# Sorted blocks loaded for two steps at a time into three places, and chosen steps in pairs

## The reference, cut to what matters

```python
h = _layernorm(x, axis=-1) * (1 + ca) + sa
x = x + ga * _L0_attn_ref(h, ...)
h = _layernorm(x, axis=-1) * (1 + cb) + sb
x = x + gb * _L0_ffn_ref(h, ...)

# _L0_ffn_ref, T = 2048 tokens of 128, 160 experts of 64
probs = jax.nn.sigmoid(x @ router_w.T + expert_bias[None, :])
top_w, top_idx = jax.lax.top_k(probs, 8)
top_w = top_w / (jnp.sum(top_w, axis=-1, keepdims=True) + 1e-09) * 2.5
combine = jnp.zeros((T, 160)).at[jnp.arange(T)[:, None], top_idx].set(top_w)
h1 = jax.nn.silu(jnp.einsum('th,eih->eti', x, w_gate))
routed = jnp.einsum('eti,ehi->th', h1 * combine.T[:, :, None], w_down)
shared = jax.nn.silu(x @ w_gate_shared.T) @ w_down_shared.T
```

## Time and profile before

| | |
|---|---|
| time, median of 3 runs | 882.31 us (877.73, 882.55, 882.31) |
| profiled execution, its time | 883.9 us |
| its span | 882.1 us |
| TensorE busy (matmuls) | 777.3 us, 88% |
| VectorE, ScalarE, GpSimd busy | 557.9, 462.4, 548.7 us |
| chain that ended last, by engine | PE 45%, POOL 16%, DVE 12%, issue 10%, ACT 10%, DMA 4%, SPq 2% |
| its largest lines | POOL wT L1370 12%, PE ps L652 10%, PE ps L639 9% |
| block loads by ScalarE (L1285) | 26 of 512 KB, median 6.2 us to landing |
| mean granted TensorE clock | 0.957 of full |

### The profile page before, as it was taken

One profiled execution on the slowest core, in us unless ns is written; L12 is line 12 of the kernel. 1 busy time (PEld: TensorE's weight loads), 2 busy tenths in 40 slices (PEclk: granted clock), 3 DMA queues, 4 the chain that ended last, 5 costly groups with the idle time before them and its releaser, 6 DMA issues.

```text
span 882.1 us, 14173 instructions
## 1 busy us (share of the span) xinstructions
PE 777.3 (88%) x4386; PEld 494.9 (56%) x4386; DVE 557.9 (63%) x1394; ACT 462.4 (52%) x965; POOL 548.7 (62%) x418
## 2 busy tenths in 40 slices
PE   4789999999989999989999887796967799799992
PEld 2556666666656666656655555444856685344440
DVE  5876676777677787677887777432432334566665
ACT  3666666666666556766767770331543444233330
POOL 0588888898878787778775783761000004777774
PEclk9899999999999999999999999686998989999997
DMA  7986958665547656445344568866999976688872
GB/s 231 244 220 179 259 131 232 187 198 151 136 121 224 183 151 163 117 109 146 90 122 123 182 216 311 265 177 239 316 386 313 384 242 200 152 192 187 188 175 57
DMA packets 81018, 174.20 MB, mean 197 GB/s; under 512 B 12448, under 2 KB 30432, under 8 KB 78640
## 3 DMA queue, kind: packets, MB, share of 16 engines
q1 hardware_dynamic: 66256, 129.96, 53.1%
q10 hardware_dynamic: 8544, 30.74, 9.4%
q0 software_dynamic: 6144, 12.60, 5.4%
HBM read 96.83 MB, written 45.48 MB: 161 GB/s over the span
## 4 chain that ended last, share of the span: by engine, by line
PE 45%; POOL 16%; DVE 12%; issue 10%; ACT 10%; DMA 4%; SPq 2%; DVEq 0%; POOLq 0%; ACTq 0%
POOL wT L1370 12%; PE ps L652 10%; PE ps L639 9%; ACT prob L1099 5%; POOL sorted_rows L1328 4%; PE ps L628 4%; PE ps L630 4%; PE ps L602 3%; PE ps L970 3%; PE ps L992 3%; PE ps L1010 3%; DVE prob L1486 3%; DMA strips<-in_expert_rows 2%; PE ps L665 2%; PE ps L613 1%
## 5 line engine op out<-in xcount | busy, mean ns | idle before, releaser
L1312 POOL TENSOR_SCALAR prob<-prob,rinv 128x512 f32<-128x512 f32 x215 | 336.6, 1575 | 101.7 <-DVE rinv L1504 99.1
L1099 ACT ACTIVATE prob<-prob,nmax 128x512 f32<-128x512 f32 x256 | 183.0, 716 | 151.2 <-DVE nmax L1486 150.7
L1370 POOL DMA_INDIRECT wT<-sorted_rows,dest x96 | 106.3, 1107 | 169.6 <-DMA sorted_rows<-prob 140.7
L1486 DVE CUSTOM_DVE_ANT_0 prob<-ps,strips 128x512 f32<-128x512 f32 x256 | 164.9, 681 | 0.9 <-issue 0.2
L639 PEld LDWEIGHTS ps<-ident,prob 128*128 128x128 f32 x1024 | 114.5, 140 | 78.9 <-POOL prob L1312 37.6
L345 DVE COPY PT<-ps 128x512 f32<-128x512 f32 x128 | 88.2, 689 | 110.8 <-PE ps L639 109.4
L639 PE MATMUL ps<-ident,prob 128*128 128x128 f32 x1024 | 136.6, 276 | 6.1 <-ACT PT L345 5.4
L652 PE MATMUL ps<-PT,v_sb 128*64 128x512 f32 x512 | 123.8, 605 | 12.9 <-ACT PT L345 12.9
L1328 POOL DMA_INDIRECT sorted_rows<-xn,dest x96 | 100.4, 1046 | 33.6 <-issue 33.6
L628 PE MATMUL ps<-stack 128*128 128x512 f32 x256 | 114.1, 446 | 6.8 <-DVE nmax L1486 6.5
L1232 ACT ACTIVATE strips<-ps 128x512 f32<-128x512 f32 x80 | 47.8, 597 | 103.9 <-PE ps L1025 103.8
(11 more groups left out here) (269 smaller groups left out, 1145.9 us busy)
## 6 DMA issues: line engine op xcount, KB each, us to landing
stack<-qk SPq DMA_DIRECT2D x128, 256.0 KB
sorted_rows<-in_zero_rows SPq DMA_DIRECT2D x16, 1024.0 KB, 5.7
wT<-sorted_rows ACTq DMA_DIRECT2D x26, 512.0 KB, 6.2
sorted_rows<-prob ACTq DMA_DIRECT2D x22, 512.0 KB, 5.7
qk<-comb_rows SPq DMA_DIRECT2D x40, 256.0 KB, 4.2
strips<-in_expert_rows SPq DMA_DIRECT2D x96, 96.0 KB, 3.6
k_low<-qk SPq DMA_DIRECT2D x64, 128.0 KB
hT<-qk SPq DMA_DIRECT2D x64, 128.0 KB
```

Source lines behind the costliest of these rows:

```text
L1099: nc.scalar.activation(prob[:, u, :], prob[:, u, :], ACT.Exp, bias=nmax[:, u:u + 1], scale=-1.0, accum_out=rsum[:, u:u + 1]).then_inc(s_ex ...
L1312: nc.gpsimd.tensor_scalar(prob[:, u, :], prob[:, u, :], rinv[:, u:u + 1], None, ALU.mult).then_inc(s_prob, 1)
L1370: nc.gpsimd.indirect_dma_start(picked[:, n % NGATHER, k, :], None, sorted_rows, bass.IndirectOffsetOnAxis(ap=dest[:, n, k:k + 1], axis=0)) ...
L1486: nc.vector.tensor_tensor_reduce(out=prob[:, u, :], in0=ps[:, BANK_S + u % 2, :], in1=backwards, scale=-1.0, scalar=3.0e38, op0=ALU.add, o ...
```

## The change

A load now brings the blocks of two steps, 2u and 2u + 1: 16 blocks, 8 KB a partition, 1 MB. `x_blocks` has three places of that size in place of six of half of it, in the same memory. SyncE issues three loads in place of six; ScalarE issues 13 in place of 26, each at the odd step 2u' + 1 whose transposes free the place. Since the blocks of both steps must be neighbours, chosen steps stand in pairs: 4, 5, 10, 11, 14, 15, 20, 21, 24, 25, 30, 31 in place of 4, 6, 9, 11, 14, 16, 19, 21, 24, 26, 29, 31. The stores stay one for each step, and the weights' four places stay. SyncE's loop goes by `CHOSEN`, so the loads of chosen weights move with it.

```diff
--- before.py
+++ after.py
@@ -67,7 +67,7 @@
 BLOCKS = E + EXTRA
 KNOWN_STEPS, CHOSEN_STEPS = E // STEP, EXTRA // STEP
 NSTEPS = KNOWN_STEPS + CHOSEN_STEPS
-CHOSEN = [4 + 5 * k // 2 for k in range(CHOSEN_STEPS)]
+CHOSEN = [s + i for s in (4, 10, 14, 20, 24, 30) for i in range(2)]
 
 
 def step_blocks():
@@ -77,7 +77,7 @@
 
 
 STEPS = step_blocks()
-NX, NCHOSEN, NY, NGATHER = 6, 4, 3, 6
+NX, NCHOSEN, NY, NGATHER = 3, 4, 3, 6
 LATE = (0, 1, 2, 3, 14, 15, 16, 17)
 RANK_UNIT = 512
 FILLS = {2: 1, 3: 1, 4: 0, 5: 0, 6: 1, 7: 2, 8: 1, 9: 1}
@@ -268,7 +268,7 @@
         scaled = prob[:, 5, :]
 
         x_flat = wT[:, :, :].rearrange("p a n -> p (a n)").bitcast(F32)
-        x_blocks = x_flat.rearrange("p (r w d) -> p r w d", r=NX, w=STEP)
+        x_blocks = x_flat.rearrange("p (r w d) -> p r w d", r=NX, w=2 * STEP)
         picked = x_flat.rearrange("p (r k d) -> p r k d", r=NGATHER, k=TOPK)
         xT = v_sb[:, :, :, :].rearrange("p a t n -> p a (t n)")
         hidden = oT
@@ -491,10 +491,10 @@
                     sp.dma_start(chosen_weights[:, k % NCHOSEN, j * 192:(j + 1) * 192],
                                  expert_rows[bass.ds(expert * P, P), :]).then_inc(s_chosen[k % NCHOSEN], 16)
 
-            def load_blocks(s):
-
-                first, _ = STEPS[s]
-                sp.dma_start(x_blocks[:, s % NX, :, :], block_rows[:, first:first + STEP, :]).then_inc(s_x[s % NX], 16)
+            def load_blocks(u):
+
+                first, _ = STEPS[2 * u]
+                sp.dma_start(x_blocks[:, u % NX, :, :], block_rows[:, first:first + 2 * STEP, :]).then_inc(s_x[u % NX], 16)
 
             def load_spread(i):
 
@@ -959,15 +959,16 @@
 
             def transpose_blocks(s):
 
-                r = s % NX
-                pe.wait_ge(s_x[r], 16 * (s // NX + 1))
+                u = s // 2
+                r = u % NX
+                pe.wait_ge(s_x[r], 16 * (u // NX + 1))
                 for half in range(2):
                     if s == 0:
                         pe.wait_ge(s_by_dve, routed(2, RANKED1))
                     else:
                         pe.wait_ge((s_xa, s_xd)[half], s)
                     for j in range(4):
-                        last = nc.tensor.transpose(ps[:, XT[half], j * P:(j + 1) * P], x_blocks[:, r, 4 * half + j, :],
+                        last = nc.tensor.transpose(ps[:, XT[half], j * P:(j + 1) * P], x_blocks[:, r, s % 2 * STEP + 4 * half + j, :],
                                                    ident[:, :])
                     last.then_inc(s_xt, 1)
 
@@ -1278,18 +1279,18 @@
                 act.wait_ge(s_yd, s + 1)
                 act.dma_start(block_rows[:, first:first + STEP, :], y_blocks[s % NY]).then_inc(s_y[s % NY], 16)
 
-            def load_blocks(s):
-
-                first, _ = STEPS[s]
-                act.wait_ge(s_xt, 2 * (s - NX + 1))
-                act.dma_start(x_blocks[:, s % NX, :, :], block_rows[:, first:first + STEP, :]).then_inc(s_x[s % NX], 16)
+            def load_blocks(u):
+
+                first, _ = STEPS[2 * u]
+                act.wait_ge(s_xt, 4 * (u - NX + 1))
+                act.dma_start(x_blocks[:, u % NX, :, :], block_rows[:, first:first + 2 * STEP, :]).then_inc(s_x[u % NX], 16)
 
             for p in range(IN_FRONT):
                 dense_silu(p)
             copy_transposed(0)
             for s in range(NSTEPS):
-                if s + NX < NSTEPS:
-                    load_blocks(s + NX)
+                if s % 2 == 1 and s // 2 + NX < NSTEPS // 2:
+                    load_blocks(s // 2 + NX)
                 block_silu(s)
                 if s >= 2:
                     store_blocks(s - 2)
```

## The result

| us | before | after |
|---|---|---|
| median of 20 runs each | 882.39 (877.73 to 887.07) | 885.62 (882.11 to 892.42) |
| profiled execution, its span | 883.9, 882.1 | 883.98, 882.1 |
| ratio after / before, 95% interval | | 1.0041 (1.0023 to 1.0059) |

The kernel became 3.6 us slower, with an interval of 2.0 to 5.2 us. Forecast were 883.0 in a range of 877 to 890, and no change within 1%: both hold.

The account below looks back on a forecast made before the run. SyncE's row of weight issues was taken to bound the steps. Start +1.3, three more issues +0.3 and one load less in front -0.6 gave +1.0 us on the median 882.3: 883 us, range 877 to 890.

Parts of the forecast that it names:

- Weights in pairs, step 24: Gate 24 waits for SyncE's 46th weight issue in place of the 43rd: +0.3 us, bounds -1.2 and +4.5.
- Start: First block load, now 1 MB, lands later and moves SyncE's row by as much: +1.3 us, bounds 0 and +1.9.
- Fewer loads in front: One ScalarE block load, 0.52 MB, less ahead of the weights at step 24: -0.6 us, bounds 0 and -1.3.
- Longer rows: Block loads with 8 KB a partition in place of 4 move no faster: 0, give or take 0.7 us.
- Steps 15 and 25, 30 and 31: Weights for 15 and 25 cost nothing; step 30 needs the 62nd issue, taken as 0, at most +1.4 us.
- two waits for chosen weights remain: Sign on TensorE: waits for chosen weights at steps 14 and 24 only.
- Waits that could appear: Block loads issued 5 steps, 14.7 us, ahead still fit; short waits for stores stay covered ahead of step 24.
- Starved weights: Rival: ScalarE's 8 KB packets take 28% of SyncE's queue turns, +6.6 us on its row; 895 us in all, chance 0.12.
- the three issues of the pair not covered (+4.5): Part of the starved rival's sum: three more weight issues ahead of step 24, in full, +4.5 us.
- Spine relieved: Rival: fewer, larger packets unblock SyncE, issues at 1.3 us in place of 1.50, step 24's wait ends; 875 us, chance 0.06.
- the gathers: Sign: GpSimd's gathers behind the steps start at 738 to 740 us.
- the end of the wait at step 24: Sign: the second wait for chosen weights, at step 24, ends at 705 to 708 us.

Follow-up runs that it names:

- run 4: Kernel before with the eight loads of combine rows moved from step 6 to step 26, behind the chosen weights: 873.25 us, ratio to before 0.9911.
- run 5: Changed kernel with the eight loads of combine rows moved from step 6 to step 26: 879.39 us, ratio to before 0.9981.
- run 7: Kernel before with 32 of the 64 weight loads, every second chosen step's, issued by GpSimd: 876.99 us, ratio to before 0.9949.
- run 8: Changed kernel with the same 32 of the 64 weight loads issued by GpSimd: 878.44 us, ratio to before 0.9971.
- run 11: Kernel before with combine rows loaded at step 26 and every second set of chosen weights issued by GpSimd: 863.93 us, ratio to before 0.9813.
- run 12: Changed kernel with combine rows loaded at step 26 and every second set of chosen weights issued by GpSimd: 865.11 us, ratio to before 0.9824.
- run 1: Kernel before with only the chosen steps changed to pairs, block loads still 0.5 MB: 885.04 us, ratio to before 1.0041.
- run 9: Kernel before with chosen steps 6, 16 and 26 moved one step earlier, to 5, 15 and 25: 884.52 us, ratio to before 1.0035.
- run 2: Changed kernel with each 1 MB load issued as two of 0.5 MB, 4 KB rows, same places and moments: 885.83 us, ratio to before 1.0046.
- run 3: Changed kernel with SyncE loading all eight weights of a pair's first step ahead of the second's: 885.24 us, ratio to before 1.0048.
- run 6: Changed kernel with the third and fifth pairs two steps later, at 16, 17 and 26, 27: 886.3 us, ratio to before 1.0057.
- run 10: Kernel before with chosen steps 9, 19 and 29 moved one step later, to 10, 20 and 30: 882.14 us, ratio to before 1.0014.

## Why the prediction was right, and which step of it failed

Right was the reading of what bounds the kernel: SyncE's row of issues decides when gate 24 opens, and all behind it follows. Experiments 4, 5, 7, 8, 11 and 12 show it, each by relieving that row; 4 and 5 take 2 MB out of the full queue besides, and in 7 and 8 the weights get a queue more, so the row is the simplest reading and not the only one for each run alone. Right were the range and "no change within 1%". The point was near by some luck: the range is 13 us wide and held the upper bound of the term that failed as well, and in the profiles a start that came out 1.5 us shorter in place of 1.3 longer hid a part of it. One term of the sum was mis-sized, and two small ones had no effect that a run shows.

**Weights in pairs, step 24: +0.3 taken, +4.0 measured.** The step said "late issues land fast, because the queue is drained while TensorE stands", and let the 46th issue land in the 3.3 us that it took before. Those 3.3 us belonged to an issue for which nobody waited: TensorE had been standing since 699.9 us, ScalarE's last transfer, a load of 0.5 MB, was issued at 699.9, and the 46th came at 702.5. In the profile after, ScalarE issued a load of 1 MB at 699.0 and a store of 0.5 MB at 700.1, the 46th came at 701.1, and TensorE stood only from 702.1. So the queue was not drained in front of it. It lands like its predecessor in that place did: 7.0 us, as the 43rd before; in experiments 1 and 9 its gate follows it by 6.4 and 7.6. With the landing alike, three more issues cost 3 x 1.3 = 3.9 us. That was the upper bound of the same paragraph ("three more issues at 1.50 us, none covered, +4.5"), with the pace of 1.3 us that the 43rd to the 46th show. Runs 1, 2 and 9 put it somewhat lower: gate 24 stands 2.9 to 3.3 us later behind line 480 than before.

**Start: +1.3 taken.** The first wait grew by 1.0 us, from 3.77 to 4.77. It was not passed on. Gates 0 and 2 stand 7.63 us apart in the profile after and 10.13 in that of before: TensorE was granted its full clock earlier, and the stretch came out 1.5 us shorter. Experiment 1, which leaves the start as it was, has the ratio of the whole change; with an interval of 2.2 us on the difference, time alone excludes neither 0 nor +1.3. The fourteen profiles say more. In the seven of kernels whose first transpose waits for the whole first 1 MB (after and runs 2, 3, 5, 6, 8 and 12) the stretch to line 480 takes 26.5 to 28.5 us, 27.1 in the mean; in the other seven 25.4 to 28.2, 27.5 in the mean. So nothing of the longer wait is seen at the end of this stretch. Gates 0 and 2 stand 7.5 to 7.9 us apart in six profiles, five of them of the first group, and 9.4 to 10.2 in the other eight: the full clock came early more often where the wait was longer. Why stays open.

**Fewer loads in front: -0.6 taken.** At step 24, for which it was taken, the landing did not become shorter: 7.0 us after, where run 1, with the same pairs and loads of 0.5 MB, has 6.4. In the 3 us ahead of the 46th issue ScalarE issued 1.5 MB, where it was 0.5 MB before. Nothing in the runs shows this term.

**Longer rows: 0 taken.** Rightly 0 in the time; runs 1 and 2 say so. From 603 to 606 us, in the first loads, the profiles of before and after have 422 and 426 GB/s, from 640 to 656 us 384 and 388. The 407 GB/s of the earlier trace rows were moved by block loads alone: only 17 of the 168 packets of that stretch have under 2 KB, so they say nothing of transfers of 96 KB, which the prediction names beside them; where weights moved too, from 640 to 656 us, the rate was 384. The Trainium skill ("DMA: Bandwidth & Descriptors", section Bandwidth) asks for 1 MiB or more in one transfer; here, with several in flight, 0.5 MB and 1 MB give the same time.

**Steps 15 and 25, 30 and 31: no cost.** That holds: no gate after 24 waited, and run 10 finds no cost in 30. **Step 20 was left out of the working**, and a wait of 3.84 us appeared there: its first loads moved back with the pair, and the 30th issue came at 680.2 us. It lies ahead of step 24 and fits into its slack, and run 1 without it has the same ratio. The sign "two waits for chosen weights remain" failed by it: there are three.

**Waits that could appear.** No transpose waited for a block after the first, so five steps ahead of its use were enough: ScalarE's 13 loads landed after 6.9 us in the middle, 11.0 at most.

**The rivals.** *Starved weights* named the mechanism that is there (1026 turns in place of 1294, an issue held for 4.76 us), and gave it a price of 6.6 us that it has not: the delay of 3.7 us at the 14th issue is still 3.6 at the 30th and shrinks to 1.2 at the 40th. These ten issues took 12.8 us in place of 15.2, in the time in which TensorE stood at step 20, and not at step 14. Whether its standing is the cause isn't shown. The other part of the rival, "the three issues of the pair not covered (+4.5)", is what happened. What it left out is that SyncE's queue carried rows of the combine table (2048 bytes a partition) in those 16 us besides the weights. *Spine relieved* did not come with the change; run 11 shows that the gain behind it is larger than the 7 us I gave it.

Of the signs, the gathers (740.6 against 738 to 740) and the end of the wait at step 24 (708.2 against 705 to 708) lie just past their range, on the side of the missing 2 to 3 us.

Open is why run 6 gained nothing, and why in run 3 the 32nd issue took 12.2 us to land (13.0 in run 5).

## What to carry to other kernels

Where consumers take from one serial row of issues, write down for each the number of the issue that it needs and the step at which it needs it. Bunching consumers leaves the row as it is and moves deadlines: at the gate where the row bound this kernel, each issue that the deadline moved back cost 1.0 to 1.3 us, nearly its full interval. Don't take for the new wait the short landing that an issue had when nobody waited for it; take the landing of the issue that was waited for in that place.

If the row is the bound, look first at what stands in it without need and at which queue is idle. Moving rows that are read much later behind the weights gave 0.9%, half of the weights on GpSimd 0.5%, both together 1.9%. With both, the edit that had cost 0.4% cost 0.1%, known to half a percent only.

## What the runs showed that was not expected

Relieving two bounds gave more than the two gains multiplied: 0.9911 x 0.9949 = 0.986, measured was 0.9813 (0.9777 to 0.9849). The product has an interval of 0.0028 of its own, so the gap of 0.0047 is barely clear of noise. Each alone leaves gates that wait 4 to 7 us (steps 19 and 24 in run 4, step 14 in run 7), and each such wait is followed by a stretch at the lower granted clock: 0.72 in the mean from 671 to 683 us in run 4, 0.79 in run 7, where run 11 has 1.00 from 657 to 700.

Two queues shared the DMA engines packet for packet at both sizes: 1246 to 1294 with rows of 4 KB, 993 to 1026 with rows of 8 KB. So one queue's longer rows take bandwidth from the other's short ones (768 bytes of weights, 2048 of the combine table): 1.35 MB in 16 us in place of 1.61. No cost of it could be told; that the loser had slack there is the likely reason.

Single profiles scatter more than the effects studied here: the first block load was issued between 596.8 and 602.3 us in the profiles of this case, all with the same program ahead of it.
